# Attention a on one Trainium2 core: q, k and V in one projection by token tiles, rotation before the transpose, and the first norm shared between two steps

## The chip, the core and the metric

The kernel runs on one core of one Trainium2 chip. The metric is the device time of one execution in microseconds (us). Before the change it is 843.65 us, the median of three runs (843.44 to 843.74). All differences below are against this kernel.

The engines are TensorE (PE in the profile, PEld for its weight loads), VectorE (DVE), ScalarE (ACT), GpSimd (POOL) and SyncE (SP, here only DMA issues). Each runs its own instructions in program order and waits for others by semaphores.

## What is computed

The input is x of 16 x 256 x 128 (16 batches, 256 tokens, width 128), all in f32. Four layers follow each other, each with a residual: attention a, an expert layer, attention b, and the expert layer again.

```python
x = x + attn_a(layernorm(x), wq, wk, wv)     # one head of width 128, rotated q and k
x = x + ffn(layernorm(x), ...)               # 8 experts of width 512, one per token by argmax
x = x + attn_b(layernorm(x), ...)            # 16 causal heads of width 64
x = x + ffn(layernorm(x), ...)               # the same experts
```

The change touches attention a and, in small things, where the second norm's output is put:

```python
q = x @ wq.T; k = x @ wk.T; v = x @ wv.T
te, to = t[..., 0::2], t[..., 1::2]          # t is q or k
re = te * cos + to * sin
ro = -te * sin + to * cos                    # interleaved again
scores = qr @ kr.T / sqrt(128)
attn = softmax(scores); return attn @ v
```

## The kernel before, in words

A batch is two token tiles of 128 tokens (TPB = 2). Attention a (`attn_a` on each engine: POOL L344, ACT L419, DVE L639, PE L1050) is a software pipeline, written out as 21 steps s = 0 to 20. In step s each engine does its part for several batches at once, always in the same written order, so the order on an engine is fixed by the source:

- batch s: first norm. VectorE takes the statistics (L605, L612, L617, tile `varA`), GpSimd makes `rstdA` from them (L317, a power of -0.5), and VectorE applies the norm to two tiles (L628, tile `lnA`) near the step's end.
- batch s - 1: TensorE transposes `lnA` (L1057), ScalarE copies it (L425, `xnT`), and TensorE projects it with `WQK`, which holds wq, wq with neighbouring columns swapped, wk, and wk swapped (L1083, four products of 256 columns; the profile counts each f32 product as two). So q and k come transposed, width on the partitions, and their swapped copies beside them. VectorE multiplies q and k with the cosines out of PSUM (L695, in the program's names `w1b<-PS,ROPE`), ScalarE copies the swapped ones (L438) and GpSimd multiplies that copy with the sines (L355, `w1b<-XY,ROPE`, 512 elements in each partition). VectorE adds both (L730, `qk<-w1b`). V is a product of its own at the end of TensorE's step (L1113), which ScalarE copies (L468).
- batch s - 2: scores (L1091), row maxima (L707, `mxa`), their negative times the scale (L718, `nba`), and exp with the row sums as a by-product (L460).
- batch s - 3: transposes of the probabilities (L1071), their copy (L433), the product with V (L1106), and the reciprocal of the sums (L664, `ria`).
- batch s - 4: residual into `X` (L657), then the statistics of the second norm (`statsF`, `mvF`, `varF`), `rstdF` on GpSimd (L317, ahead of `rstdA` in the same step), VectorE's bias `nbF` (L699), ScalarE's normalised tiles `lnF` (L447).
- batch s - 5: ScalarE copies `lnF` into `TOK` (L453), from which the rows are later scattered to the experts; transposes (L1040) and the router's product (L1046), logits (L635).

VectorE's whole step from s = 4 on, in order: L657 (X), L664 (ria), L605 of batch s (statsA), L605 of s - 4 (statsF), L612 (mvF), L612 (mvA), L617 (varF), L617 (varA), L695 (cosines), L699 (nbF), L707 (mxa), L635 (logits), L718 (nba), L628 (lnA), L730 (the add). GpSimd's: rstdF, rstdA, L355. From s = 13 to 15 the 28 instructions of the first routing are woven into VectorE's steps at marked places (`part()`), and from s = 15 on GpSimd issues the scatters (L322) behind its step. TensorE gets 20 idle products at the start and some in steps 18 to 20 (`keep_clock`, L1035). The expert layer follows.

Of the kernel before, what the change touches and what calls it, by code (L numbers as in the profile page):

```python
# [34 lines left out]
SCALE_A = float(1.0 / np.sqrt(np.float32(D)))  # L35
# [55 lines left out]

def expert_steps(step, first=0, beside=None):
# [11 lines left out]
def build(nc, ids, x, wqk_a, wv_a, rope, w_q, w_k, wv_b, w_o, W1, b1t, W2, b2, Wr, br, cst, out):  # L104
    ctx = ExitStack()
    with ctx:
# [33 lines left out]
        for n in "AFB":  # L140
# [3 lines left out]
                "out": LN["A"]["out"] if n == "B" else sb(f"ln{n}", [P, 2, TPB, D]),  # L144
# [15 lines left out]
        va = sb("va", [P, 2, TPB, D])  # L160
        nbF = sb("nbF", [P, 2, TPB])
        mxa, nba, rsa, ria = (sb(n, [P, 2, TPB]) for n in ("mxa", "nba", "rsa", "ria"))
# [54 lines left out]
        (a_xT_ps, a_xT, a_qk_ps, a_qks, a_sin, a_rot, a_rope, a_v_ps, a_v, a_scores, a_max, a_nb, a_exp, a_rinv, a_pT_ps, a_pT,  # L217
         a_out_ps, a_x) = (sem("a_" + n) for n in (
             "xT_ps", "xT", "qk_ps", "qks", "sin", "rot", "rope", "v_ps", "v", "scores", "max", "nb", "exp", "rinv", "pT_ps", "pT",
             "out_ps", "x"))  # L220

        r_xT_ps, r_xT, r_tok, r_lg_ps, r_lg = (sem("r_" + n) for n in ("xT_ps", "xT", "tok", "lg_ps", "lg"))
# [27 lines left out]
        def _(sp):  # L250
# [57 lines left out]
        def _(pool):  # L308
# [17 lines left out]
            def before_scatters(k):  # L326
                pool.wait_ge(r_step, STEPS * (k + 1))
                pool.wait_ge(r_tok, GB * (k + 1))
                pool.wait_ge(s_xs0, 64)
# [14 lines left out]
            def attn_a(s, u):  # L344
                if has(s - 4):
                    rstd(LN["F"], s - 4, u)
                if has(s):
                    rstd(LN["A"], s, u)
                b = s - 1
                if has(b):  # L350
                    pool.wait_ge(a_qks, b + 1)
                    wait(pool, a_rope, b)
                    if fixed(b) and b == 0:
                        pool.wait_ge(s_wa, 48)
                    nc.gpsimd.tensor_tensor(rot[:, 1, :], qks[:, :], ROPE[:, 1, :], ALU.mult).then_inc(a_sin, 1)  # L355

            peeled(attn_a, 0, ROUTE0_AT - 1)
# [13 lines left out]
            def attn_b(s, u, more=None):  # L371
                hb, fb, gb, v = s - 1, s - 2, s - 3, (u + 1) % 2
                for q in range(QUADS):
# [39 lines left out]
        def _(act):  # L413
# [5 lines left out]
            def attn_a(s, u, beside=None):  # L419
                v = (u + 1) % 2  # L420
                b = s - 1
                if has(b):
                    act.wait_ge(a_xT_ps, b + 1)
                    wait(act, a_v_ps, b - 1)
# [17 lines left out]
                if has(b):  # L442

                    act.wait_ge(s_nbF, b + 1)
                    wait(act, r_xT_ps, b - 1)
                    for i in range(TPB):
                        last = nc.scalar.activation(LN["F"]["out"][:, u, i, :], X[:, ds(TPB * b + i), :], ACT.Identity,  # L447
                                                    bias=nbF[:, u, i:i + 1], scale=LN["F"]["rstd"][:, u, i:i + 1])
                    last.then_inc(LN["F"]["s_out"], 1)
                b = s - 5  # L450
                if has(b):
                    act.wait_ge(LN["F"]["s_out"], b + 1)
                    nc.scalar.copy(TOK[:, ds(TPB * b, TPB), 0:D], LN["F"]["out"][:, v, :, :]).then_inc(r_tok, 1)  # L453
                b = s - 2
                if has(b):
                    act.wait_ge(a_nb, b + 1)
                    wait(act, a_pT_ps, b - 1)
                    wait(act, a_rinv, b - 1)
                    for i in range(TPB):
                        last = nc.scalar.activation(pa[:, u, i, :], PS[:, 2, i * M:(i + 1) * M], ACT.Exp,  # L460
                                                    bias=nba[:, u, i:i + 1], scale=SCALE_A,
                                                    accum_out=rsa[:, u, i:i + 1])
                    last.then_inc(a_exp, 1)
                b = s - 1
                if has(b):
                    act.wait_ge(a_v_ps, b + 1)
                    wait(act, a_out_ps, b - 1)
                    nc.scalar.copy(va[:, v, :, :], PS[:, 5, 0:TPB * D].rearrange("p (t d) -> p t d", t=TPB)).then_inc(a_v, 1)  # L468
# [128 lines left out]
        def _(dve):  # L597
            nc.vector.memset(idle[:, :], 0.0).then_inc(s_idle, 1)
# [26 lines left out]
            def norm_apply(ln, n, tile, slot):  # L625
                dve.wait_ge(ln["s_rstd"], n + 1)
                for i in range(TPB):
                    last = nc.vector.tensor_scalar(ln["out"][:, slot, i, :], X[:, ds(tile + i), :],  # L628
# [10 lines left out]
            def attn_a(s, u, parts=()):  # L639
# [6 lines left out]
                if fixed(s) and s == 0:  # L646
                    dve.wait_ge(s_x0, 16)
                if fixed(s) and s == 2:
                    dve.wait_ge(s_x1, 16)
                if fixed(s) and s == 4:  # L650
                    dve.wait_ge(s_x2, 16)
                b = s - 4
                if has(b):
                    dve.wait_ge(a_out_ps, b + 1)
                    dve.wait_ge(a_rinv, b + 1)
                    for i in range(TPB):
                        last = nc.vector.scalar_tensor_tensor(  # L657
                            out=X[:, ds(TPB * b + i), :], in0=PS[:, 6, i * D:(i + 1) * D], scalar=ria[:, u, i:i + 1],
                            in1=X[:, ds(TPB * b + i), :], op0=ALU.mult, op1=ALU.add)
                    last.then_inc(a_x, 1)  # L660
                b = s - 3
                if has(b):
# [724 lines left out]
```

## Time and profile before

| what | value |
|---|---|
| median of three runs | 843.65 us |
| the profiled execution's own time | 843.43 us |
| its span, first to last instruction | 841.6 us |
| TensorE busy, mean granted clock | 798.5 us (95%), 0.994 |
| VectorE, ScalarE, GpSimd busy | 620.1, 566.4, 436.7 us |
| 22619 instructions | 6860 products on TensorE |

Times in all views are us from the span's start. A busy TensorE is not a TensorE at its peak, since its products are pipelined and their ends are modelled. Idle time of an engine matters only where its instruction is the last that something waits for. Attention a fills about the first 115 us of the span, attention b the stretch from some 230 to 730 us, the two expert layers the rest.

### The profile page before, as it was taken

Reading aid. Unit: us, or ns where it says so; the run is one execution under the profiler, and the core shown is the slowest. Engines: PE = TensorE matmul, PEld = TensorE weight load, DVE = VectorE, ACT = ScalarE, POOL = GpSimd, SP = SyncE. Lnnn points to the kernel's source line nnn. Section 1 sums busy time; section 2 is a strip of 40 time slices with the busy share of each in tenths; the row PEclk is TensorE's granted clock in tenths of the full one; section 3 lists DMA queues with packets and bytes.
Section 4 is the critical chain, followed back from the end, with each engine's and each line's share of the span. In section 5 each row is a group of like instructions: output and inputs, shape, how many; then the busy total and the mean of one; then the engine's idle time right before and its main releaser. Section 6 shows DMA issues by size and latency. Waiting matters only on the chain.

```text
span 841.6 us, 22619 instructions
## 1 busy us (share of the span) xinstructions
PE 798.5 (95%) x6860; PEld 691.8 (82%) x6860; DVE 620.1 (74%) x2697; ACT 566.4 (67%) x2044; POOL 436.7 (52%) x771
## 2 busy tenths in 40 slices
PE   7999869999899999999999999999999999899993
PEld 5888738999788888888888888888778888589992
DVE  4889766667667777777777777887767777576665
ACT  2676635666677777777777777767767777356661
POOL 3343655677544544544544444444884444237772
PEclk9999999999999999999999999999999999999997
DMA  9930021313200000000000000000020000003135
GB/s 322 336 124 2 16 76 65 118 54 99 70 2 2 2 2 2 2 2 2 2 2 2 2 2 2 2 3 1 27 96 5 2 2 3 1 23 124 54 102 168
DMA packets 26358, 40.45 MB, mean 48 GB/s; under 512 B 4672, under 2 KB 18112, under 8 KB 25216
## 3 DMA queue, kind: packets, MB, share of 16 engines
q1 hardware_dynamic: 19136, 27.71, 10.1%
q0 software_dynamic: 4992, 10.27, 3.8%
q8 instruction: 56, 0.92, 0.5%
q10 hardware_dynamic: 2112, 1.05, 0.5%
q14 instruction: 62, 0.51, 0.2%
HBM read 20.58 MB, written 18.43 MB: 46 GB/s over the span
## 4 chain that ended last, share of the span: by engine, by line
PE 74%; DVE 9%; POOL 7%; issue 5%; DMA 2%; ACT 1%; DVEq 1%; SPq 0%; POOLq 0%
PE PS L1192 11%; PE PS L1204 10%; PE PS L1183 10%; PE PS L1156 9%; PE PS L1147 9%; PE PS L1235 6%; PE PS L1028 5%; PE PS L1030 5%; PE PS L1029 5%; POOL xs_dram L322 3%; POOL w1b L355 2%; PE PS L1139 1%; POOL rstdA L317 1%; POOL pb L381 1%; DVE qk L730 1%
## 5 line engine op out<-in xcount | busy, mean ns | idle before, releaser
L379 POOL TENSOR_SCALAR pb<-pb,rib 128x128 f32<-128x128 f32 x256 | 95.3, 372 | 247.0 <-DVE rib L907 246.4
L898 DVE CUSTOM_DVE_ANT_0 PS<-PS,CST 128x128 f32<-128x128 f32 (+1 forms) x512 | 169.0, 382 | 60.5 <-PE PS L1204 60.5
L912 DVE COPY pT<-PS 128x384 f32<-128x384 f32 x256 | 140.1, 554 | 37.8 <-PE PS L1183 37.6
L523 ACT ACTIVATE pb<-PS,nbb 128x128 f32<-128x128 f32 x256 | 94.9, 371 | 96.1 <-DVE nbb L898 92.3
L496 ACT ACTIVATE yT<-PS,w1b 128x128 f32<-128x128 f32 x368 | 104.9, 368 | 61.0 <-PE PS L1147 61.0
L381 POOL TENSOR_SCALAR pb<-pb,rib 128x256 f32<-128x256 f32 x256 | 122.3, 478 | 0.0
L1183 PE MATMUL PS<-CST,pb 128*128 128x128 f32 x768 | 117.5, 278 | 4.4 <-POOL pb L381 3.9
L525 ACT ACTIVATE pb<-PS,nbb 128x256 f32<-128x256 f32 x256 | 121.2, 473 | 0.0
L1183 PEld LDWEIGHTS PS<-CST,pb 128*128 128x128 f32 x768 | 85.9, 142 | 28.0 <-issue 23.0
L338 POOL DMA_INDIRECT yt_dram<-XY x92 | 90.7, 986 | 32.6 <-issue 24.4
L1192 PE MATMUL PS<-pT,vb 128*64 128x256 f32 (+1 forms) x1024 | 103.2, 339 | 2.1 <-DVE pT L912 1.8
L1204 PE MATMUL PS<-qk 64*128 64x128 f32 (+1 forms) x1024 | 101.3, 337 | 0.0
L1156 PE MATMUL PS<-yT 128*128 128x128 f32 x736 | 97.5, 275 | 0.5 <-ACT yT L496 0.3
L1147 PE MATMUL PS<-pb,w1b 128*128 128x128 f32 x736 | 97.4, 275 | 0.4 <-issue 0.4
L1192 PEld LDWEIGHTS PS<-pT,vb 128*64 128x64 f32 x1024 | 62.2, 136 | 39.7 <-ACT qk L532 9.1
L532 ACT COPY qk<-PS 128x512 f32<-128x512 f32 x128 | 75.6, 591 | 25.9 <-PE PS L1030 25.5
L1156 PEld LDWEIGHTS PS<-yT 128*128 128x128 f32 x736 | 89.6, 192 | 1.0 <-ACT yT L496 0.9
L322 POOL DMA_INDIRECT xs_dram<-TOK,POS x64 | 65.6, 1026 | 47.1 <-DVE xs L850 29.0
L1147 PEld LDWEIGHTS PS<-pb,w1b 128*128 128x128 f32 x736 | 89.4, 192 | 0.6 <-issue 0.6
L1204 PEld LDWEIGHTS PS<-qk 64*128 64x128 f32 x1024 | 72.5, 187 | 14.0 <-issue 10.8
L1028 PE MATMUL PS<-xh,WQKh 128*128 128x256 f32 x256 | 77.8, 304 | 0.9 <-ACT qk L532 0.9
L1030 PE MATMUL PS<-xh,WQKl 128*128 128x256 f32 x256 | 72.5, 283 | 0.0
(134 smaller groups left out, 1690.9 us busy)
## 6 DMA issues: line engine op xcount, KB each, us to landing
xs_dram<-XY SPq DMA_DIRECT2D x4, 1483.5 KB, 13.1
XY<-xs_dram SPq DMA_DIRECT2D x4, 1225.5 KB, 6.1
W1S<-in_W SPq DMA_DIRECT2D x1, 2048.0 KB, 20.3
W2S<-in_W SPq DMA_DIRECT2D x4, 512.0 KB, 8.1
out_dram<-X SPq DMA_DIRECT2D x6, 256.0 KB, 2.4
yt_dram<-XY POOLq DMA_INDIRECT x92, 2.6
XY<-xs_dram SPq DMA_DIRECT2D x4, 258.0 KB, 2.6
xs_dram<-TOK,POS POOLq DMA_INDIRECT x64, 2.3
```

What stands on the lines that cost most here:

```text
L381: nc.gpsimd.tensor_scalar(pb[:, i, P:3 * P], pb[:, i, P:3 * P], rib[:, i, 1:2], 1.0, ALU.mult, ALU.mult).then_inc(b_p, 1)
L496: last = nc.scalar.activation(hT[:, v, c, :], PS[:, v, c * P:(c + 1) * P], ACT.Gelu, bias=w1b1[:, v, F + c:F + c + 1])
L525: nc.scalar.activation(pb[:, r, P:3 * P], PS[:, bank, P:3 * P], ACT.Exp, bias=nbb[:, r, 1:2], scale=-1.0, accum_out=rsb[:, r, 1:2]).then_i ...
L898: last = nc.vector.tensor_tensor_reduce(ps, ps, CST[:, m:m + c1 - c0], -SCALE_B, HIGHEST, ALU.add, ALU.min, nbb[:, hh % 4, c0 // P:c0 // P ...
L912: nc.vector.tensor_copy(pT[:, hh % 4, :], PS[:, bank, 0:3 * P]).then_inc(b_pT, 1)
L1028: mm(ps, one_pass(lhs[0]), one_pass(rhs[0]), start=True, stop=False)
L1030: return mm(ps, one_pass(lhs[1]), one_pass(rhs[0]), start=False, stop=True)
L1147: last = mm(PS[:, v, c * P:(c + 1) * P], w1b1[:, v, c * P:(c + 1) * P], xsT[:, v, :], start=True, stop=True)
L1156: last = mm(PS[:, 6 + w, 0:D], hT[:, w, c, :], w2b2[:, r, c * D:(c + 1) * D], start=c == 0, stop=c == FC - 1)
L1183: last = tr(PS[:, bank, c * P:(c + 1) * P], pb[:, hh % 4, c * P:(c + 1) * P], ident)
L1192: last = mm(PS[i * DK:(i + 1) * DK, bank, k0:M], vb[:, v if b is hb else u, c, hh * DK:(hh + 1) * DK], pT[:, hh % 4, a0:a1], start=c == 0, ...
L1204: last = mm(PS[:, S_BANKS[2 * half + i], c0:c0 + k1], qk[r, half, 0, q0:q0 + P], qk[r, half, 1, 0:k1], start=True, stop=True)
```

## The change

Projection: for each token tile one product of 384 columns with `WQKV` (wq, wk, wv side by side, the even columns of q and k ahead of the odd ones) gives q, k and V with the tokens on the partitions. The swapped copies of the weights are gone; the two halves of a row take their part. ScalarE copies q and k of both tiles (512 elements) out of PSUM; VectorE multiplies this copy in SBUF with the cosines, GpSimd makes the sine part from it in two instructions of 256 elements, VectorE adds. The sum is then transposed on TensorE (four transposes, at the beginning of the next step), copied by ScalarE, and only then come the scores. The scale is in the tables, so the maxima are negated at once and `nba` as an own instruction goes. V has a column of ones, so that the product with V gives the row sums in its last column (129 columns); their reciprocal moves to the beginning of the next step.

Norm: the statistics of batch s + 1 are taken in step s, and the norm of batch s is applied at the beginning of step s. A step s = -1 is put in front. The second norm's output goes straight into `TOK` in both attentions; the copies L453 and L387 go.

VectorE's step after, in order: reciprocal, lnA of batch s (two), statsA of s + 1 (two), X (two), statsF (two), mvF, mvA, varF, varA, nbF, negated maxima, cosines, logits, add. GpSimd's: rstdF, rstdA of s + 1, sines (two). TensorE's: transposes of lnA (s - 1), of TOK (s - 5), of the probabilities (s - 3), of q and k (s - 2), projection (s - 1), scores (s - 2), router (s - 5), product with V (s - 3).

```diff
-            sp.dma_start(WQK[:, :, :], wqk_a).then_inc(s_wa, 16)
-            sp.dma_start(ROPE[:, :, :], rope).then_inc(s_wa, 16)
+            sp.dma_start(WQKV[:, :], wqkv_a).then_inc(s_wa, 16)
+            sp.dma_start(ROPE[:, :, :, :], rope).then_inc(s_wa, 16)
             sp.dma_start(X[:, 4:8, :], xv[:, 4:8, :]).then_inc(s_x1, 16)
-            sp.dma_start(WVA[:, :], wv_a).then_inc(s_wa, 16)
...
# GpSimd, attn_a
-                if has(s):
-                    rstd(LN["A"], s, u)
+                if has(s + 1):
+                    rstd(LN["A"], s + 1, (s + 1) % 2)
                 b = s - 1
                 if has(b):
                     pool.wait_ge(a_qks, b + 1)
                     wait(pool, a_rope, b)
...
-                    nc.gpsimd.tensor_tensor(rot[:, 1, :], qks[:, :], ROPE[:, 1, :], ALU.mult).then_inc(a_sin, 1)
+                    for h in range(2):
+                        last = nc.gpsimd.tensor_tensor(by_halves(rot[:, 1, :])[:, :, :, h, :],
+                                                       by_halves(qks)[:, :, :, 1 - h, :],
+                                                       ROPE[:, 1 + h, :, None, :].to_broadcast([P, TPB, 2, D // 2]), ALU.mult)
+                    last.then_inc(a_sin, 1)
...
# ScalarE, attn_a, behind the copy of the transposed probabilities
+                b = s - 2
+                if has(b):
+                    act.wait_ge(a_qkT_ps, b + 1)
+                    wait(act, a_scores, b)
+                    nc.scalar.copy(qkT.rearrange("p w m -> p (w m)"), PS[:, 5, :]).then_inc(a_qkT, 1)
                 b = s - 1
                 if has(b):
-                    act.wait_ge(a_qk_ps, b + 1)
+                    act.wait_ge(a_qkv_ps, b + 1)
                     wait(act, a_sin, b)
-                    nc.scalar.copy(qks[:, :], PS[:, 1, :]).then_inc(a_qks, 1)
+                    wait(act, a_rot, b)
+                    nc.scalar.copy(qks.rearrange("p (t c) -> p t c", t=TPB), PS[:, 0:TPB, 0:2 * D]).then_inc(a_qks, 1)
...
-                    nc.scalar.copy(TOK[:, ds(TPB * b, TPB), 0:D], LN["F"]["out"][:, v, :, :]).then_inc(r_tok, 1)
...
                         last = nc.scalar.activation(pa[:, u, i, :], PS[:, 2, i * M:(i + 1) * M], ACT.Exp,
-                                                    bias=nba[:, u, i:i + 1], scale=SCALE_A,
-                                                    accum_out=rsa[:, u, i:i + 1])
+                                                    bias=nba[:, u, i:i + 1])
...
# VectorE, attn_a (a = s + 1, f = s - 4)
+                if has(f):
+                    dve.wait_ge(a_out_ps, f + 1)
+                    out_ps = PS[:, 6, 0:TPB * DI].rearrange("p (t d) -> p t d", t=TPB)
+                    nc.vector.reciprocal(ria[:, u, :], out_ps[:, :, D]).then_inc(a_rinv, 1)
+                if has(s):
+                    if s >= 2:
+                        dve.wait_ge(a_xT_ps, s - 1)
+                    norm_apply(LN["A"], s, TPB * s, u)
+                if has(a):
+                    bn_stats(LN["A"], a, TPB * a, a % 2)
+                if has(f):
+                    dve.wait_ge(a_rinv, f + 1)
                     for i in range(TPB):
                         last = nc.vector.scalar_tensor_tensor(
-                            out=X[:, ds(TPB * b + i), :], in0=PS[:, 6, i * D:(i + 1) * D], scalar=ria[:, u, i:i + 1],
+                            out=X[:, ds(TPB * f + i), :], in0=out_ps[:, i, 0:D], scalar=ria[:, u, i:i + 1],
...
                     dve.wait_ge(a_x, f + 1)
                     bn_stats(LN["F"], f, TPB * f, u)
...
-                    dve.wait_ge(a_qk_ps, b + 1)
-                    nc.vector.tensor_tensor(rot[:, 0, :], PS[:, 0, :], ROPE[:, 0, :], ALU.mult).then_inc(a_rot, 1)
                 part()
                 if has(f):
                     dve.wait_ge(LN["F"]["s_rstd"], f + 1)
...
-                    nc.vector.reduce_max(mxa[:, u, :], PS[:, 2, :].rearrange("p (t m) -> p t m", t=TPB),
-                                         AX.X).then_inc(a_max, 1)
+                    nc.vector.reduce_max(nba[:, u, :], PS[:, 2, :].rearrange("p (t m) -> p t m", t=TPB),
+                                         AX.X, negate=True).then_inc(a_nb, 1)
                 part()
+                b = s - 1
+                if has(b):
+                    dve.wait_ge(a_qks, b + 1)
...
+                    nc.vector.tensor_tensor(rot[:, 0, :].rearrange("p (t g c) -> p t g c", t=TPB, g=4),
+                                            qks.rearrange("p (t g c) -> p t g c", t=TPB, g=4),
+                                            ROPE[:, 0, :, None, :].to_broadcast([P, TPB, 4, D // 2]),
+                                            ALU.mult).then_inc(a_rot, 1)
...
-                    nc.vector.tensor_scalar(nba[:, u, :], mxa[:, u, :], -SCALE_A, None, ALU.mult).then_inc(a_nb, 1)
                 part()
-                if has(s) and not (fixed(s) and s == 1):
...
-                    norm_apply(LN["A"], s, TPB * s, u)
...
# TensorE, attn_a, behind the transposes of the probabilities
+                b = s - 2
+                if has(b):
+                    pe.wait_ge(a_rope, b + 1)
+                    wait(pe, a_qkT, b)
+                    for i in range(TPB):
+                        for w in range(2):
+                            last = tr(PS[:, 5, w * M + i * P:w * M + (i + 1) * P], qkn[:, (2 * i + w) * D:(2 * i + w + 1) * D],
+                                      ident)
+                    last.then_inc(a_qkT_ps, 1)
...
-                    for i in range(2):
-                        for w in range(2):
-                            last = mm(PS[:, i, w * M:(w + 1) * M], WQK[:, 2 * w + i, :], xnT[:, v, :],
-                                      start=True, stop=True)
-                    last.then_inc(a_qk_ps, 1)
+                    wait(pe, a_v, b)
+                    for i in range(TPB):
+                        last = mm(PS[:, i, 0:3 * D], xnT[:, v, i * P:(i + 1) * P], WQKV[:, :], start=True, stop=True)
+                    last.then_inc(a_qkv_ps, 1)
...
```

## Rows read from the trace of the kernel before

**Rows 1.** The stages in windows: us and count by engine, clock, DMA share, GB/s.

```profile
40.00:60.00 20.00, 19.92 (x126) 17.39 (x125) 17.44 (x78) 13.98 (x43) 7.69 (x10) 1.00 0.53 161
...
100.00:120.00 20.00, 13.46 (x79) 8.21 (x78) 10.69 (x41) 11.56 (x28) 14.12 (x16) 1.00 0.13 40
```

**Rows 2.** Chain of waits and VectorE timeline: the add that ends steps 3, 12, 16.

```profile
22.89 0.60 DVE qk L730
...
74.01 0.60 DVE qk L730
...
98.51 0.69 DVE L730 TENSOR_TENSOR qk<-w1b 128x512 f32<-128x512 f32 x1
```

**Rows 3.** VectorE in order of time through step 7: start us, us, line, operands.

```profile
39.61 0.68 DVE L730 TENSOR_TENSOR qk<-w1b 128x512 f32<-128x512 f32 x1
...
40.22 0.60 DVE L657 SCALAR_TENSOR_TENSOR X<-PS,ria,X 128x128 f32<-128x128 f32 x2
...
40.81 0.46 DVE L605 BATCH_NORM_STATS2 statsA<-X 128x6 f32<-128x128 f32 x2
...
41.19 0.46 DVE L605 BATCH_NORM_STATS2 statsF<-X 128x6 f32<-128x128 f32 x2
...
41.80 0.25 DVE L612 BATCH_NORM_AGGREGATE mvF<-statsF 128x2 f32<-128x6 f32 x2
...
42.16 0.17 DVE L617 TENSOR_SCALAR varF<-mvF 128x2 f32<-128x2 f32 x1
...
43.47 0.15 DVE L699 SCALAR_TENSOR_TENSOR nbF<-mvF,rstdF 128x2 f32<-128x2 f32 x1
...
43.72 0.69 DVE L707 TENSOR_REDUCE mxa<-PS 128x2 f32<-128x512 f32 x1
...
44.45 0.38 DVE L718 TENSOR_SCALAR nba<-mxa 128x2 f32<-128x2 f32 x1
...
44.74 0.59 DVE L628 TENSOR_SCALAR lnA<-X,mvA,rstdA 128x128 f32<-128x128 f32 x2
...
45.25 0.68 DVE L730 TENSOR_TENSOR qk<-w1b 128x512 f32<-128x512 f32 x1
```

**Rows 4.** GpSimd in order of time through the same step.

```profile
42.41 0.69 POOL L317 TENSOR_TENSOR rstdF<-varF,half 128x2 f32<-128x2 f32 x1 [3.25 <-DVE varF L617]
...
43.06 0.69 POOL L317 TENSOR_TENSOR rstdA<-varA,half 128x2 f32<-128x2 f32 x1
...
43.71 1.09 POOL L355 TENSOR_TENSOR w1b<-XY,ROPE 128x512 f32<-128x512 f32 x1
```

**Rows 5.** TensorE and ScalarE in order of time in the same step.

```profile
40.83 1.99 PE L1083 MATMUL PS<-xnT,WQK 128*128 128x256 f32 x8
...
42.66 1.03 PE L1091 MATMUL PS<-qk 128*128 128x256 f32 x4
...
44.86 0.61 PE L1113 MATMUL PS<-WVA,xnT 128*128 128x128 f32 x4
...
42.86 0.59 ACT L438 COPY XY<-PS 128x512 f32<-128x512 f32 x1 [1.29 <-PE PS L1083]
```

**Rows 6.** VectorE and GpSimd side by side in step 14.

```profile
85.16 0.29 DVE L784 TENSOR_TENSOR r_exc<-r_ps,r_exc 128x128 f32<-128x128 f32 x1
...
85.38 1.09 POOL L355 TENSOR_TENSOR w1b<-XY,ROPE 128x512 f32<-128x512 f32 x1
...
85.97 0.64 DVE L785 TENSOR_TENSOR r_exc<-r_exc,r_hot 128x128 f32<-128x128 f32 x1
```

**Rows 7.** Costliest groups: GpSimd on 128 and on 256 elements.

```profile
L379 POOL TENSOR_SCALAR pb<-pb,rib 128x128 f32<-128x128 f32 x256 | 95.3, 372 | 247.0 <-DVE rib L907 246.4
...
L381 POOL TENSOR_SCALAR pb<-pb,rib 128x256 f32<-128x256 f32 x256 | 122.3, 478 | 0.0
```

**Rows 8.** The start in order of time.

```profile
8.24 0.37 ACT L425 COPY xnT<-PS 128x256 f32<-128x256 f32 x1 [6.23 <-PE PS L1057]
...
9.52 1.99 PE L1083 MATMUL PS<-xnT,WQK 128*128 128x256 f32 x8 [1.31 <-DMA WVA<-in_wv_a]
```

More of the change, by code:

```diff
@@ L159, in build @@
         qk = sb("qk", [P, 2, 2, M])
-        va = sb("va", [P, 2, TPB, D])
+        qkn, qkT = qk[:, 0].rearrange("p a m -> p (a m)"), qk[:, 1]
+        va = sb("va", [P, 2, TPB, D + 1])
         nbF = sb("nbF", [P, 2, TPB])
-        mxa, nba, rsa, ria = (sb(n, [P, 2, TPB]) for n in ("mxa", "nba", "rsa", "ria"))
+        nba, ria = (sb(n, [P, 2, TPB]) for n in ("nba", "ria"))
         pa = lent[:, 0:2 * TPB * M].rearrange("p (a b m) -> p a b m", a=2, b=TPB)
@@ L423, in attn_a @@
                     act.wait_ge(a_xT_ps, b + 1)
-                    wait(act, a_v_ps, b - 1)
+                    wait(act, a_qkv_ps, b - 1)
                     nc.scalar.copy(xnT[:, v, :], PS[:, 4, 0:M]).then_inc(a_xT, 1)
@@ L444, in attn_a @@
                     act.wait_ge(s_nbF, b + 1)
[L445 removed]
                     for i in range(TPB):
[L447 removed]
+                        last = nc.scalar.activation(TOK[:, TPB * b + i, 0:D], X[:, ds(TPB * b + i), :], ACT.Identity,
                                                     bias=nbF[:, u, i:i + 1], scale=LN["F"]["rstd"][:, u, i:i + 1])
                     last.then_inc(LN["F"]["s_out"], 1)
[L450 to L453 removed]
                 b = s - 2
@@ L627, in norm_apply @@
                 for i in range(TPB):
-                    last = nc.vector.tensor_scalar(ln["out"][:, slot, i, :], X[:, ds(tile + i), :],
+                    to = TOK[:, tile + i, 0:D] if ln is LN["F"] else ln["out"][:, slot, i, :]
+                    last = nc.vector.tensor_scalar(to, X[:, ds(tile + i), :],
                                                    ln["mv"][:, slot, i, 0:1], ln["rstd"][:, slot, i:i + 1],
@@ L675, in attn_a @@
                 part()
-                if has(s):
-                    bn_aggr(LN["A"], s, u)
+                if has(a):
+                    bn_aggr(LN["A"], a, a % 2)
                 part()
@@ L682, in attn_a @@
                 part()
-                if has(s):
-                    norm_var(LN["A"], s, u)
+                if has(a):
+                    norm_var(LN["A"], a, a % 2)
                 part()
-                if fixed(s) and s == 1:
-                    norm_apply(LN["A"], s, TPB * s, u)
-                b = s - 1
-                if has(b):
-                    dve.wait_ge(a_qk_ps, b + 1)
-                    if fixed(b) and b == 0:
-                        dve.wait_ge(s_wa, 48)
-                    wait(dve, a_rope, b)
-                    nc.vector.tensor_tensor(rot[:, 0, :], PS[:, 0, :], ROPE[:, 0, :], ALU.mult).then_inc(a_rot, 1)
                 part()
@@ L728, in attn_a @@
                     dve.wait_ge(a_sin, b + 1)
-                    wait(dve, a_scores, b - 1)
-                    nc.vector.tensor_tensor(qk[:, v, :, :].rearrange("p a m -> p (a m)"), rot[:, 0, :], rot[:, 1, :],
-                                            ALU.add).then_inc(a_rope, 1)
+                    wait(dve, a_qkT_ps, b)
+                    nc.vector.tensor_tensor(qkn, rot[:, 0, :], rot[:, 1, :], ALU.add).then_inc(a_rope, 1)
                 part()
@@ L1105, in attn_a @@
                         for kc in range(TPB):
-                            last = mm(PS[:, 6, i * D:(i + 1) * D], pTa[:, v, kc, i * P:(i + 1) * P],
+                            last = mm(PS[:, 6, i * DI:(i + 1) * DI], pTa[:, v, kc, i * P:(i + 1) * P],
                                       va[:, v, kc, :], start=kc == 0, stop=kc == TPB - 1)
                     last.then_inc(a_out_ps, 1)
-                b = s - 1
-                if has(b):
-                    wait(pe, a_v, b)
-                    for i in range(TPB):
-                        last = mm(PS[:, 5, i * D:(i + 1) * D], xnT[:, v, i * P:(i + 1) * P], WVA[:, :],
-                                  start=True, stop=True)
-                    last.then_inc(a_v_ps, 1)
             def route(k):
@@ L1355 @@
     a = {n.replace("L0_", ""): np.asarray(v) for n, v in inputs.items()}
-    swap = np.arange(D) ^ 1
-    wq, wk = a["attn_a_wq"].T, a["attn_a_wk"].T
+    halves = np.concatenate([np.arange(0, D, 2), np.arange(1, D, 2)])
     rope, cst = tables()
```

97 lines of the change are left out of this document (39 added, 58 removed).

## The prediction, made before the changed kernel was seen

> **What bounds the kernel now.** The windows come first: through attention a TensorE is busy 19.92 of 20 us, later in the stage, where it is busy 13.46 of 20 us, its granted clock is still 1.00 [rows 1]. That looks like a stage bound by TensorE, but the chain of waits does not run over TensorE there. It goes from VectorE's add L730 through VectorE's own step to GpSimd (rstdF, rstdA, L355) and back to L730, once for each step. The adds that close steps 3 and 12 stand at 22.89 and 74.01, the one of step 16 at 98.51 [rows 2]: 5.68 us a step up to step 12.
>
> The timelines of step 7 show the loop. From the add's issue at 39.61 to varF at 42.16 VectorE takes 2.55 us without a hole; GpSimd starts rstdF 0.25 later, then come 0.65, 0.65 and 1.09 us, to 44.80; the add follows 0.45 later, at 45.25 [rows 3, 4]. The sum is 5.64, the whole step. One row says why GpSimd's end matters before the add: L718, a tiny VectorE instruction, lasts 0.38 us and ends at 44.83, just behind L355 at 44.80 [rows 3, 4]. Behind it stand only lnA (0.51) and the add. TensorE's step is as long because two loops are nearly equal: its own instructions fill 5.5 to 5.6 us.
>
> Attention b and the experts hardly touch what is changed: a copy on GpSimd and a wait there go, on engines that are not their limit. I count them at nothing, with 0.5 us either way as my bound.
>
> **TensorE, part by part.** The projection goes from 2048 to 1536 moving columns in all. Eight products took 1.83 us (40.83 to 42.66), so I take 1.83 x 0.75 = 1.37 us. V's four (up to 0.61) go, and four new transposes of 128 columns come, for which the same row stands as a bound [rows 5]; I take 0.55 for each. Net: 0.46 us less in each step, some 5.2 in place of 5.6. This is off the path unless the other loop shrinks as well.
>
> **VectorE and GpSimd, where the step is decided.** Let the add be issued at 0. All durations are those of step 7 [rows 3, 4] unless said.
>
> - To the next instruction 0.61. The reciprocal 0.07 (it stood between X and statsA and only moves). lnA, now here, 0.51. statsA 0.38.
> - X is 0.60 long, and statsF now stands directly behind it and needs its result. Such a wait on its own result costs 0.15 more: statsF ends at 41.65, and mvF is issued at 41.80. Before, ria and statsA stood in between. So 0.75, of which 0.23 is new.
> - statsF to mvF 0.61, mvF to varF 0.36. varF is issued at 3.29.
> - GpSimd: rstdF at 3.54, rstdA at 4.19, the sines at 4.84.
> - VectorE meanwhile has nothing between varA and nbF, for the cosines no longer stand there. rstdF ends at 4.23, nbF comes 0.2 later at 4.43, the maxima at 4.53, the cosines can be issued at 5.14.
> - The sines are two instructions of 256 elements. If they only share the old work they take 1.09 together. On GpSimd going from 128 to 256 elements adds 0.106 to 0.372 us [rows 7], so a second start can cost up to 0.27: 1.36. I take 1.25, nearer to the upper end because the halves are also taken in runs of 64 elements.
>
> Do sines and cosines run side by side? The cosines read q and k from SBUF now, not PSUM, so both factors lie in SBUF. Step 14 has such a pair: L785, two SBUF inputs, is issued during L355, lasts 0.64 us in place of the 0.29 of its like L784, and ends at 86.61, 0.14 behind L355's end at 86.47 [rows 6]. L718 shows the same hold [rows 3]. So I take them one behind the other: 4.84 + 1.25 + 0.55 for the cosines' elements, and 0.2 until the add is issued. That gives 6.84, rounded 6.8 us a step, whichever of the three instructions goes first.
>
> The Trainium skill (SBUF — State Buffer, "Who interferes with whom") states this as a rule: a VectorE instruction with two SBUF inputs contends with a GpSimd instruction that reads SBUF, and whoever comes second is blocked to the other's end. The trace agrees with L355 and not with rstdA: nbF, with two SBUF inputs, ran at 43.47 inside rstdA's 43.06 to 43.75. By the rule the step is 6.8, without it 6.3.
>
> Could anything else be later than this? After the add (0.68 busy and 0.06) TensorE transposes q and k (0.55), projects (1.37, end 0.16 later), ScalarE copies q and k (0.05 and 0.59): the copy is ready at 3.5, the scores at 3.7 [rows 5]. Both are earlier than the sines at 4.84 and the maxima at 4.53. The new copies on ScalarE (0.59 for the transposed q and k) stand beside a removed one and two removed reads of the sums; ScalarE stays below 4.5 us of work. So a step with the second norm lasts 6.8, a step without it is set by this path: 3.5 + 1.25 + 0.55 + 0.2 = 5.5.
>
> **The start.** The first projection waited for V's weights until 9.52 although its operand was copied at 8.61 [rows 8]. Those bytes go, and I expect it at 8.7: a gain of 0.85. It ends 1.53 later, at 10.2, the copy at 10.85, sines and cosines 2.0 later: first add at 12.85. Steps 2 and 3 at 5.5 bring it to 23.85, against 22.89: the gain is lost again, 1.0 late, because the transposes stand in front of the projection now and wait for the add.
>
> **The sum.** Steps 4 to 12: 9 x 6.8 = 61.2, so the add of step 12 stands at 85.05, 11.0 later than 74.01. In steps 13 to 15 routing instructions stand in front of nbF and fill its wait; what is left is statsF's wait and the shared reads. I take 0.5 for each of the steps 13 to 16, bounded by 0.1 and 1.1 (the whole difference of the steps before). That is 2.0. In the last four steps the reciprocal has no cover any more (about 0.25 each), and a copy of about as much goes from ScalarE: nothing, with 1 us either way. Together 13.0 us. The profiled execution took 843.43, its span 841.6; 843.4 + 13.0 = 856.4. The median of the runs is 0.2 above that execution, which I neglect.
>
> **Rivals.**
>
> 1. *Sines and cosines do not hold each other up.* For it: nbF inside rstdA. Against it: L785 and L718. Then the step is the later of 4.84 + 1.25 + 0.2 = 6.3 and 5.14 + 0.69 + 0.15 = 5.98. First add 12.3, steps 2 and 3 at 4.95, step 12's add at 22.2 + 56.7 = 78.9, 4.9 late; with 1.0 for steps 13 to 16 this gives 849.3. With sines at 1.09 it is 6.13 a step, and 847.8.
> 2. *The other side: TensorE set the step, and gets shorter.* For it: busy 19.92 of 20 us [rows 1]. Saved would be 0.46 in each of 15 steps, 6.9, and 0.85 at the start: 835.6. It decides only if the loop over VectorE and GpSimd closes in less than 5.2 us, and for no loss at all it must close within the present 5.64. My sum has 6.13 as its lowest, and the same sum gave the old step to the hundredth. I would have to be wrong about lnA or nbF.
> 3. *A half costs GpSimd as much as the whole*, because of the exchanged halves and the broadcast table. Then the sines take 2.18, the step 7.7, and with the steps around it the time is about 867. No row speaks for it, only the lack of such a pattern in the trace.
>
> **How the numbers follow.** The main case gets 0.62; its own range is 854 to 859 (6.65 to 7.0 a step, and 1 us for the end). Rival 1 gets 0.22, rival 2 0.08, rival 3 0.05. The last 0.03 is for gains at the ends that cancel the loss. The range 848 to 860 holds the main case and nearly all of rival 1. A change under 0.2%, 1.7 us, is not told from none here: faster 0.09, same 0.03, slower 0.88.
>
> **What would show it.** Right: adds of VectorE 6.8 apart in steps 5 to 12; a hole of about 0.9 on VectorE before nbF, ended by rstdF; cosines longer than their 0.69, ending behind a GpSimd instruction; TensorE idle before the transposes of q and k, waiting for the add; busy for some 5.2 us in each step, with the clock at 1.00; first projection at 8.7. Wrong: adds less than 6.1 apart, cosines of 0.69 beside the sines (rival 1), or no idle time on TensorE (rival 2).

## The result, and the profile after

The changed kernel takes 856.37 us, the median of four runs (855.73 to 857.73); the kernel before took 843.69 us beside it (843.44 to 844.88). The ratio is 1.0148, with a 95% interval from 1.0135 to 1.0160: slower by 12.7 us. The prediction was 856.4 us. The experiments were run in three batches. In the second one the kernel before took 889.37 us, with a lower granted clock in the expert layers (0.93 in 120 to 240 us in all_split, 1.00 in all_split_again, the same kernel in the third batch). Both batches ran on chip 8, and what lowered the clock is open. Each experiment is therefore read by its ratio to the kernel before in its own batch, and by the steps of attention a, which agree between the batches (5.69 and 5.68 us for cos_hole, 5.43 twice for all_split). The ratios are estimated over all runs and can differ from the quotient of two medians by up to 0.001.

The page of the kernel after, its span and the busy time of each engine:

```profile
span 854.0 us, 22411 instructions
...
PE 794.6 (93%) x6793; PEld 679.0 (80%) x6796; DVE 622.4 (73%) x2682; ACT 567.9 (66%) x2012; POOL 438.3 (51%) x771
```

The span grew by 12.4 us while TensorE's work shrank by 3.9 us and no other engine's grew by more than 2.3. The page alone does not show the loss: it lies in waits.

The kernel after in windows, with the columns of [rows 1]:

```profile
10.00:15.00 5.00, 1.29 (x8) 1.02 (x8) 2.88 (x12) 1.42 (x4) 2.27 (x3) 0.98 1.07 380
15.00:20.00 5.00, 3.73 (x12) 2.28 (x11) 2.04 (x4) 1.77 (x5) 1.92 (x3) 0.67 1.01 425
...
40.00:60.00 20.00, 15.44 (x95) 12.28 (x94) 15.15 (x60) 12.54 (x30) 8.97 (x12) 0.98 0.43 137
...
100.00:105.00 5.00, 4.87 (x20) 3.38 (x18) 3.88 (x20) 2.48 (x6) 1.04 (x2) 0.66 0.01 3
```

In 40 to 60 us TensorE is busy 15.44 us where it was 19.92 [rows 1]. With a step of 6.64 us that is 5.13 us a step. The granted clock, which was 1.00 in this stage before, falls in three short stretches, to means of 0.67, 0.74 (60 to 65 us) and 0.66 over 5 us. Such a mean mixes the two levels, 2.4 GHz at 1.00 and 1.2 GHz at 0.50.

The timeline of the kernel after, all engines: the start, then steps 6 and 7, then the add of step 12, two rows of step 15, and the add of step 16. Columns are start, length, engine, line, operands.

```profile
8.13 1.53 PE L1095 MATMUL PS<-WQKV,xnT 128*128 128x384 f32 x4 [0.55 <-ACT xnT L432]
...
10.58 1.08 POOL L322 TENSOR_TENSOR rstdA<-varA,half 128x2 f32<-128x2 f32 x1 [1.79 <-DVE varA L623]
...
12.97 0.69 DVE L733 TENSOR_TENSOR qk<-w1b 128x512 f32<-128x512 f32 x1 [1.85 <-POOL w1b L362]
...
18.70 0.68 DVE L717 TENSOR_TENSOR w1b<-XY,ROPE 128x512 f32<-128x512 f32 x1
...
24.63 0.69 DVE L733 TENSOR_TENSOR qk<-w1b 128x512 f32<-128x512 f32 x1
...
42.77 1.07 DVE L717 TENSOR_TENSOR w1b<-XY,ROPE 128x512 f32<-128x512 f32 x1
...
43.25 1.09 POOL L362 TENSOR_TENSOR w1b<-XY,ROPE 128x256 f32<-128x256 f32 x1
...
44.43 0.69 DVE L733 TENSOR_TENSOR qk<-w1b 128x512 f32<-128x512 f32 x1 [0.51 <-issue]
...
45.18 0.66 PE L1085 MATMUL PS<-CST,qk 128*128 128x128 f32 x4 [0.32 <-DVE qk L733]
...
47.74 0.17 DVE L623 TENSOR_SCALAR varF<-mvF 128x2 f32<-128x2 f32 x1
...
47.99 0.69 POOL L322 TENSOR_TENSOR rstdF<-varF,half 128x2 f32<-128x2 f32 x1 [3.65 <-DVE varF L623]
48.65 0.69 POOL L322 TENSOR_TENSOR rstdA<-varA,half 128x2 f32<-128x2 f32 x1
48.72 0.16 DVE L700 SCALAR_TENSOR_TENSOR nbF<-mvF,rstdF 128x2 f32<-128x2 f32 x1 [0.71 <-POOL rstdF L322]
...
49.30 1.69 POOL L362 TENSOR_TENSOR w1b<-XY,ROPE 128x256 f32<-128x256 f32 x2
49.41 1.07 DVE L717 TENSOR_TENSOR w1b<-XY,ROPE 128x512 f32<-128x512 f32 x1
...
50.62 0.44 PE L1042 MATMUL PS<-CST,TOK 128*128 128x128 f32 x2 [1.07 <-DVE LG L643]
51.07 0.69 DVE L733 TENSOR_TENSOR qk<-w1b 128x512 f32<-128x512 f32 x1 [0.51 <-issue]
...
84.69 0.69 DVE L733 TENSOR_TENSOR qk<-w1b 128x512 f32<-128x512 f32 x1 [0.51 <-issue]
...
101.57 2.46 PE L1095 MATMUL PS<-WQKV,xnT 128*128 128x384 f32 x4
...
104.06 0.59 ACT L451 COPY XY<-PS 128x512 f32<-128x512 f32 x1 [1.67 <-PE PS L1095]
...
111.94 0.69 DVE L733 TENSOR_TENSOR qk<-w1b 128x512 f32<-128x512 f32 x1
```

How to read it. The adds L733 stand 6.64 us apart (44.43 to 51.07), where L730 stood 5.64 apart [rows 3]. Counted from the add, varF comes at 3.31, rstdF at 3.56, rstdA at 4.22 and the sines at 4.87. The two sines fill 1.69 us, to 50.99, and the add follows 0.08 later. The cosines last 1.07 in place of the 0.68 that they took at 18.70, where no GpSimd instruction stood beside them (the sines of that step ended at 18.27). The step before shows the order inside. The cosines (42.77 to 43.84) end behind the first sine, and the second sine, issued at 43.25, lasts 1.09 us and ends at 44.34, 0.50 behind the cosines. So the three run one at a time: sine, cosines, sine. The chain of waits of the same step, kernel after, says it in its own way:

```profile
49.34 1.15 POOL w1b L362 x2
...
50.56 0.51 issue
```

### The profile page after: what moved, and what is told of

Its sections match the earlier page's. It is cut to its first block, busy times and chain, and to the rows that moved or that the text cites. A ratio compares the mean times of both kernels' runs of the same rounds, so it can differ in the third digit from the quotient of the medians.

```text
span 854.0 us, 22411 instructions
## 1 busy us (share of the span) xinstructions
PE 794.6 (93%) x6793; PEld 679.0 (80%) x6796; DVE 622.4 (73%) x2682; ACT 567.9 (66%) x2012; POOL 438.3 (51%) x771
## 3 DMA queue, kind: packets, MB, share of 16 engines
q1 hardware_dynamic: 18992, 27.25, 9.9%
## 4 chain that ended last, share of the span: by engine, by line
PE 72%; DVE 9%; POOL 8%; issue 7%; DMA 1%; ACT 1%; DVEq 1%; POOLq 0%; SPq 0%
PE PS L1196 10%; PE PS L1208 10%; PE PS L1187 10%; PE PS L1151 9%; PE PS L1160 9%; PE PS L1239 6%; PE PS L1030 5%; PE PS L1032 5%; PE PS L1031 5%; POOL xs_dram L327 3%; POOL w1b L362 2%; PE PS L1143 1%; POOL rstdA L322 1%; POOL pb L391 1%; DVE X L677 1%
## 5 line engine op out<-in xcount | busy, mean ns | idle before, releaser
L900 DVE DVE_READ_ACCUMULATOR2_ANT nbb<- 128x1 f32 x512 | 72.5, 142 | 0.0
```

The source lines that it names most:

```text
L900: last = nc.vector.tensor_tensor_reduce(ps, ps, CST[:, m:m + c1 - c0], -SCALE_B, HIGHEST, ALU.add, ALU.min, nbb[:, hh % 4, c0 // P:c0 // P ...
```

## The experiments

All edits are against the kernel after, but for the first, which is against the kernel before.

**norm_only**: the norm part alone, put into the kernel before.

```diff
-  (VectorE, at the step's end)   norm_apply(LN["A"], s, ...)
+  (VectorE, first in the step)   norm_apply(LN["A"], s, ...); bn_stats(LN["A"], s + 1, ...)
-  (GpSimd)                       rstd(LN["A"], s, u)
+  (GpSimd)                       rstd(LN["A"], s + 1, (s + 1) % 2)
```

> The kernel before with only the norm's part of the change: statistics of batch s + 1 in step s, the norm applied at the beginning of step s. Theory (the loop over VectorE and GpSimd sets the step): from the add 0.61, lnA 0.51, statsA 0.38, X and the wait of statsF for it 0.75, 0.61, 0.36, so varF at 3.22; GpSimd 0.25, 0.65, 0.65, 1.09, and 0.2 to the add: 6.0 a step in place of 5.64. Nine full steps and a little in steps 13 to 16: 847.5 us (846 to 849). Rival (lnA behind the sines was the cost, its move is a gain, and the loss of the change comes from the projection alone): 5.2 to 5.6 a step, 839 to 844 us.

Measured: 849.76 us (847.78 to 851.49) beside 843.53, ratio 1.0074 (1.0054 to 1.0094). VectorE and GpSimd in time through step 7:

```profile
41.80 0.69 DVE L728 TENSOR_TENSOR qk<-w1b 128x512 f32<-128x512 f32 x1
...
46.59 1.09 POOL L355 TENSOR_TENSOR w1b<-XY,ROPE 128x512 f32<-128x512 f32 x1
...
46.99 0.72 DVE L720 TENSOR_SCALAR nba<-mxa 128x2 f32<-128x2 f32 x1
...
47.78 0.69 DVE L728 TENSOR_TENSOR qk<-w1b 128x512 f32<-128x512 f32 x1
```

The step is 5.98, as expected. lnA stood behind GpSimd before, and it stands ahead of varF now. With it and with statsF's wait for X, varF is issued 3.24 behind the add, where it was 2.55; at the other end the add follows L355's end by 0.10 and no longer by 0.45. L720, which has two elements in a partition, lasts 0.72 us and ends with L355. The time is above what the step alone makes: steps 4 to 12 give 2.6 us, the rest comes at the start (1.2) and in steps 13 to 16 (1.6); the add of step 16 stands at 103.80, 5.3 late.

**proj_only**: the projection part alone, the norm where it was.

```diff
-                if has(s + 1):
-                    rstd(LN["A"], s + 1, (s + 1) % 2)
+                if has(s):
+                    rstd(LN["A"], s, u)
...
+                if has(s) and s != 1:          # VectorE, behind the logits, ahead of the add
+                    norm_apply(LN["A"], s, TPB * s, u)
```

> The changed kernel with the norm as it was before (statistics of batch s in step s, lnA behind the logits); the projection, the rotation and the row sums as changed. Theory: lnA goes from the beginning of the step, where it costs 0.5, to behind the sines, where it costs the same, since its VectorE instruction does not start before GpSimd is through; the step stays 6.5 to 6.7, the time 854 to 858 us. Rival (the moved norm is what costs): 845 to 850 us.

Measured: 857.37 us (853.5 to 858.89) beside 843.53, ratio 1.0161 (1.0128 to 1.0193). VectorE through step 7:

```profile
44.07 0.68 DVE L735 TENSOR_TENSOR qk<-w1b 128x512 f32<-128x512 f32 x1
...
49.60 0.83 DVE L636 TENSOR_SCALAR lnA<-X,mvA,rstdA 128x128 f32<-128x128 f32 x2
50.35 0.68 DVE L735 TENSOR_TENSOR qk<-w1b 128x512 f32<-128x512 f32 x1
```

A step of 6.28, less than I expected: lnA lies in the time in which the add waits for the held sine anyway, so it costs little there. The nine steps are 3.6 us shorter than in the kernel after. The time is not, because steps 13 to 15 take 22.5 us (81.78 to 104.26) where the kernel after takes 21.9, its add of step 3 is 0.7 later, and the 2.2 us that its add of step 16 (109.74) is ahead are lost behind it. In the step the two parts add up: 0.34 for the norm and 0.64 for the projection, of 1.00 for both. In the time they do not. The step to the third add takes 7.33 us here, with a clock of 0.86 and 0.79 in 15 to 25 us, and step 15 takes 7.56, with 0.71 in 95 to 100 us; idle2 below shows what such falls cost. So moving the norm back alone is no cure.

**cos_psum**: the cosines read q and k from PSUM again, beside ScalarE's copy.

```diff
-                                            qks.rearrange("p (t g c) -> p t g c", t=TPB, g=4),
+                                            PS[:, 0:TPB, 0:2 * D].rearrange("p t (g c) -> p t g c", g=4),
...
+                    act.wait_ge(a_rot, b + 1)     # the copy of V and the next projection wait for the cosines
+                    wait(pe, a_rot, b)
```

> The changed kernel, only that VectorE multiplies q and k with the cosines out of PSUM, behind ScalarE's copy of them, so that one of its two factors is not in SBUF; ScalarE's copy of V waits for it. Theory (cosines and sines hold each other up, about 0.5 us in each step): cosines 0.69 long, the two sines without a hole between them, step 6.1; 0.53 in each of 16 steps less at most, 848 to 851 us. Rival (no hold, the cosines only come late): step 6.6, 856 us as changed.

Measured: 850.04 us (847.76 to 851.19) beside 843.53, ratio 1.0070 (1.0051 to 1.0088). VectorE and GpSimd through step 7:

```profile
43.98 0.69 DVE L734 TENSOR_TENSOR qk<-w1b 128x512 f32<-128x512 f32 x1 [0.45 <-issue]
...
48.84 1.24 POOL L362 TENSOR_TENSOR w1b<-XY,ROPE 128x256 f32<-128x256 f32 x2
48.96 0.68 DVE L718 TENSOR_TENSOR w1b<-PS,ROPE 128x512 f32<-128x512 f32 x1
...
50.17 0.69 DVE L734 TENSOR_TENSOR qk<-w1b 128x512 f32<-128x512 f32 x1 [0.46 <-issue]
```

With one input in PSUM, cosines and sines run side by side: 0.68 and 1.24 us, nothing held, a step of 6.19. The hold is worth 0.45 us a step. By the medians of the two batches this one operand is worth half of the whole loss (6.3 of 12.7 us); the nine steps 4 to 12 give 4.0 of it, steps 13 to 16 another 1.4, and the start gives nothing (the add of step 3 stands at 25.52, again with a fall of the clock, 0.66 in 15 to 20 us).

**idle2**: two idle products of 512 columns behind TensorE's work in steps 1 to 12.

```diff
+                if 1 <= s < ROUTE0_AT:
+                    keep_clock(2, 4)
```

> The changed kernel with two idle products of 512 columns at the end of TensorE's step, in steps 1 to 12: 0.43 us more work for TensorE in each. Theory (TensorE has over 1 us free in a step of 6.64): the step stays 6.64, and the three falls of the granted clock (stretches at 0.67, 0.74 and 0.66) become fewer; 854 to 856.5 us. Rival (TensorE sets the step): 0.43 more in 12 steps, 861 us.

Measured: 855.03 us (854.75 to 856.6) beside 843.53, ratio 1.0141 (1.0124 to 1.0158). VectorE's adds, at the start and in step 7:

```profile
13.82 0.69 DVE L733 TENSOR_TENSOR qk<-w1b 128x512 f32<-128x512 f32 x1 [1.85 <-POOL w1b L362]
...
19.03 0.69 DVE L733 TENSOR_TENSOR qk<-w1b 128x512 f32<-128x512 f32 x1
...
44.05 0.69 DVE L733 TENSOR_TENSOR qk<-w1b 128x512 f32<-128x512 f32 x1 [0.50 <-issue]
...
50.70 0.69 DVE L733 TENSOR_TENSOR qk<-w1b 128x512 f32<-128x512 f32 x1 [0.51 <-issue]
```

More work on TensorE, and the same step of 6.65: TensorE does not set it. The clock's falls moved and did not go: the three of the kernel after are not there, others stand at 90 to 95 us (0.66) and 115 to 125 us (0.88, 0.78). That gives their price, since the same steps are now seen at 1.00. The step to the second add takes 5.21 us where it took 6.44 with the clock at 0.67, the step to the third is the same in both (5.21 and 5.22), and step 15 takes 5.94 (in cos_psum too) where it took 6.64 with 0.66. So the falls cost 1.23 and 0.70 us there. Not every fall costs time: step 14, in which idle2 has its fall, takes 7.45 us, and 7.44 without one, and the step of the kernel after that holds the fall at 60 to 65 us takes 6.69, against 6.64 in idle2.

**hole**: lnA put into VectorE's wait for rstdF, behind varA.

```diff
-                if has(s):                        # first in VectorE's step
-                    norm_apply(LN["A"], s, TPB * s, u)
...
                     norm_var(LN["A"], a, a % 2)
+                if has(s):
+                    norm_apply(LN["A"], s, TPB * s, u)
```

> The changed kernel, only that lnA of batch s stands behind varA, in VectorE's wait for rstdF, not at the beginning of the step. Theory: the 0.50 of lnA leaves the way from the add to varF (3.31 to 2.81) and is hidden in the wait of 0.71 before nbF; the step goes from 6.64 to 6.14, the time to 850 us (848.5 to 852). Rival (lnA is held up by GpSimd's rstdF, as L718 was by L355, or the wait does not hide it): the step stays above 6.4, 853 us or more.

Measured: 895.99 us (895.06 to 897.45) beside 889.37, ratio 1.0081 (1.0057 to 1.0105). VectorE and GpSimd through step 7:

```profile
43.89 0.69 DVE L733 TENSOR_TENSOR qk<-w1b 128x512 f32<-128x512 f32 x1 [0.51 <-issue]
...
46.88 0.60 DVE L636 TENSOR_SCALAR lnA<-X,mvA,rstdA 128x128 f32<-128x128 f32 x2
46.94 0.69 POOL L322 TENSOR_TENSOR rstdF<-varF,half 128x2 f32<-128x2 f32 x1 [3.14 <-DVE varF L623]
...
47.66 0.16 DVE L700 SCALAR_TENSOR_TENSOR nbF<-mvF,rstdF 128x2 f32<-128x2 f32 x1 [0.18 <-POOL rstdF L322]
...
50.02 0.69 DVE L733 TENSOR_TENSOR qk<-w1b 128x512 f32<-128x512 f32 x1 [0.51 <-issue]
```

A step of 6.13. The hole of 0.71 before nbF becomes 0.18; lnA at the head of the step costs its whole 0.51.

**cos_hole** and **cos_hole_again**: both edits together, in the second batch and once more in the third.

> Both edits on the changed kernel: the cosines out of PSUM, and lnA in the wait before nbF. Theory (both costs lie in one loop and add): 2.81 + 0.25 + 0.65 + 0.65 + 1.24 + 0.09 = 5.69 a step, 844.5 us (843 to 846), as the kernel before. Rival (TensorE's order becomes the bound once the loop is shorter): 5.9 or more a step, 846 to 849 us.

> Both edits (cosines out of PSUM, lnA in the wait before nbF) beside the changed kernel on one chip. Theory: 5.69 a step, so the loss of 1.5% is gone but for 0.2%; the two edits together are worth 1.3 to 1.5%. Rival (half of the loss lies elsewhere): 0.5% or more over the kernel before.

Measured: 890.03 us beside 889.37, ratio 1.0000 (0.9985 to 1.0014), and 843.86 (843.11 to 845.97) beside 844.02, ratio 0.9995 (0.9981 to 1.0010). VectorE's adds in the repeat:

```profile
38.72 0.69 DVE L734 TENSOR_TENSOR qk<-w1b 128x512 f32<-128x512 f32 x1 [0.46 <-issue]
...
44.40 0.69 DVE L734 TENSOR_TENSOR qk<-w1b 128x512 f32<-128x512 f32 x1 [0.45 <-issue]
```

5.68 us a step, the step of the kernel before. The savings in the step add up (0.45 and 0.51, together 0.96 of 6.64), and the whole loss of 1.5% is gone. The nine steps give 8.7 us of it. 2.8 come at the start, where the clock does not fall here and the add of step 3 stands at 21.80 and not 24.63, and 1.5 in steps 13 to 16. The clock is 1.00 in 15 to 20 us in both runs, while hole alone has 0.53 and cos_psum alone 0.66; why is open.

**cos_hole_sin**: in addition rstdA behind the sines on GpSimd, since its reader lnA now comes a step later.

```diff
-                if has(s + 1):
-                    rstd(LN["A"], s + 1, (s + 1) % 2)     # ahead of the sines
...
+                if has(s + 1):
+                    rstd(LN["A"], s + 1, (s + 1) % 2)     # behind them
```

> As cos_hole, and GpSimd makes rstdA of batch s + 1 behind the sines, since lnA needs it only in the next step. Theory: rstdA's 0.65 leaves GpSimd's part of the loop (5.04), and VectorE's own way is the longest now: varF at 2.81, then 0.98 to nbF, 0.08, 0.61, and 0.84 for the cosines and the wait for them: 5.3 a step; 840.5 us (839 to 842.5), faster than both kernels. Rival (GpSimd's place in the loop does not matter, something else holds the step at 5.65): 844 us.

Measured: 890.10 us (888.57 to 892.75) beside 889.37, ratio 1.0014 (1.0001 to 1.0027). VectorE and GpSimd in step 7:

```profile
48.02 1.23 POOL L360 TENSOR_TENSOR w1b<-XY,ROPE 128x256 f32<-128x256 f32 x2
48.09 0.58 DVE L701 SCALAR_TENSOR_TENSOR nbF<-mvF,rstdF 128x2 f32<-128x2 f32 x1
```

A miss: 5.59 a step (38.39 to 43.98), not 5.3. The sines start 0.65 earlier and hold nbF: two SBUF inputs, two elements, 0.58 us in place of 0.16, until the first sine ends. Maxima and cosines stand behind it. The time does not follow the step at all: step 12 ends 1.02 earlier than in cos_hole (72.26 against 73.28), and step 13 alone gives 0.86 back (8.23 against 7.37).

**all_split** and **all_split_again**: in addition the second half of statsA between X and statsF, where statsF waited for X.

```diff
                     last.then_inc(a_x, 1)
+                    if has(a):
+                        stats_a(1).then_inc(LN["A"]["s_stats"], 1)
                     dve.wait_ge(a_x, f + 1)
```

> As cos_hole_sin, and statsA's second half stands between X and statsF, so that statsF does not wait for a result just made. Theory: 0.2 less on the same way, 5.1 a step, where TensorE's own 5.2 takes over: 839.5 us (838 to 842). Rival (TensorE is the bound already in cos_hole_sin): no difference from it, 840.5 us.

> All four edits. Theory: adds 5.43 apart, 0.3 to 0.5% under the kernel before. Rival (the gain of before belongs to that chip, where the expert layers run otherwise): no difference from the kernel before.

Measured: 886.41 us (883.71 to 887.77) beside 889.37, ratio 0.9966 (0.9952 to 0.9979), and 839.64 (839.4 to 841.84) beside 844.02, ratio 0.9951 (0.9936 to 0.9967). VectorE and GpSimd of the repeat, in steps 6 and 7, and one row of step 13:

```profile
43.72 1.23 POOL L360 TENSOR_TENSOR w1b<-XY,ROPE 128x256 f32<-128x256 f32 x2
43.76 0.62 DVE L707 SCALAR_TENSOR_TENSOR nbF<-mvF,rstdF 128x2 f32<-128x2 f32 x1 [0.19 <-POOL rstdF L322]
...
45.61 0.69 DVE L740 TENSOR_TENSOR qk<-w1b 128x512 f32<-128x512 f32 x1
...
51.04 0.69 DVE L740 TENSOR_TENSOR qk<-w1b 128x512 f32<-128x512 f32 x1
...
77.22 1.14 DVE L767 TENSOR_TENSOR r_hot<-CST,r_best 128x128 bf16<-128x128 f32 x1
```

5.43 a step, with nbF still held (I had hoped for 5.1). This version beats the kernel before by 0.3 to 0.5%, and with that the kernel after by some 2%. Step 13 gives part back: 72.74 to 80.77, 8.03 us. lnA and r_hot now stand beside the sines (76.59 to 77.82) and last 0.99 and 1.14 us, and the clock is 0.86 and 0.79 in 75 to 85 us; the two were not told apart.

**all_nb**: in addition nbF's product on GpSimd, from means negated on VectorE in front of varF.

```diff
+                    nc.vector.tensor_scalar(nmF[:, u, :], LN["F"]["mv"][:, u, :, 0], -1.0, None, ALU.mult)
...
+                    nc.gpsimd.tensor_tensor(nbF[:, u, :], nmF[:, u, :], LN["F"]["rstd"][:, u, :],
+                                            ALU.mult).then_inc(s_nbF, 1)
```

> As all_split, and nbF is no longer a VectorE instruction with two SBUF inputs beside the sines: VectorE negates the means before varF, GpSimd multiplies them with rstdF, behind it. Theory (nbF was held by the first sine and lasted 0.62 in place of 0.16): VectorE's step loses the hold, GpSimd's gets one small instruction of about 0.2; adds 5.2 apart, where TensorE's own work ends, 2 us less than all_split. Rival (nbF was late for another reason, or GpSimd's small instruction costs as much): 5.4 apart, no difference.

Measured: 842.86 us (839.24 to 843.9) beside 844.02, ratio 0.9977 (0.9963 to 0.9991). Its VectorE timeline has the add of step 16 3.4 us earlier than all_split_again (99.19); the window at the start of the experts follows:

```profile
95.82 0.69 DVE L741 TENSOR_TENSOR qk<-w1b 128x512 f32<-128x512 f32 x1 [0.19 <-issue]
```

```profile
126.00:128.00 2.00, 2.00 (x10) 1.48 (x8) 1.48 (x5) 0.00 (x0) 1.70 (x2) 0.50 0.12 38
```

The steps are 5.27 apart, as expected, but the time is a miss: not shorter than all_split's. In this profile the granted clock is 0.50, the level of 1.2 GHz, just when the experts begin (eight products at 126.91 last 1.84 us, eight of the same at 128.99 in all_split_again 1.07). That goes with the loss. So do the ten runs: the three shortest (839.24 to 840.73) have a mean clock of 0.989 or 0.990, the other seven (842.31 to 843.90) 0.987. Whether the clock explains all of it stays open.

**after_again**: the kernel after in the third batch.

> The changed kernel as it is, on the chip of the following three, so that the steps of the ladder are compared on one chip. Theory: 1.5% over the kernel before, adds 6.64 apart. Rival (the 1.5% belongs to the first chip): another ratio.

Measured: 857.13 us (857.04 to 859.66) beside 844.02, ratio 1.0162 (1.0140 to 1.0184), adds 6.64 apart. The result stands.

## Why the prediction was right

The time and the mechanism were right. That the time is met to 0.1 us is luck, though: the terms of the sum were off by 0.7 to 1.1 us each, two of them one way and two the other. Adds are taken from the timelines, where those of steps 3 and 12 before stand at 22.81 and 73.93, 0.08 earlier than in the chain's rows [rows 2].

| term | predicted, later by | measured |
|---|---|---|
| up to the add of step 3 | 1.0 | 1.8 (24.63 against 22.81) |
| steps 4 to 12 | 10.0 (6.8 a step) | 8.9 (60.06 against 51.12; 6.67 a step) |
| steps 13 to 16 | 2.0 | 2.7 (27.25 against 24.58) |
| behind step 16 | 0 (1 either way) | -1.0 |
| span | 13.0 | 12.4 |

- *The front of the loop*: right to 0.03. varF, rstdF, rstdA and the sines were put at 3.29, 3.54, 4.19 and 4.84 and came at 3.31, 3.56, 4.22 and 4.87. lnA ahead of varF and the wait of statsF for X cost what they were put at; the hole on VectorE before nbF was 0.71 and not about 0.9. What the order costs is shown by hole: with lnA in that hole the step is 0.51 shorter.
- *The hold*: right, and shown by cos_psum. The Trainium skill (SBUF — State Buffer, "Who interferes with whom") says that a VectorE instruction with two SBUF inputs and a reading GpSimd instruction exclude each other, the later one being blocked. The rows agree for sines and cosines, and for nbF beside a sine (0.58 and 0.62 us). For rstdA they agree in one order only. nbF took 0.16 inside it (48.65 to 49.34). But rstdA is itself blocked when the cosines come first: it lasts 1.08 us at 10.58, issued 0.16 behind them, and 0.69 in cos_psum, where they read PSUM.
- *Its size* was put 0.1 too high: 0.55 expected, 0.45 by cos_psum. The order I left open is sine, cosines, sine. The sines themselves were put at 1.25 and take 1.24 wide. And the add is issued 0.08 behind GpSimd's end, not 0.2. These, less the 0.03 of the front, make 6.64 out of 6.84.
- *Rival 1* (no hold, 6.3 or 6.13 a step) is the kernel cos_psum, and there the step is 6.19. So its sum was right too, for a kernel that is not this one.
- *Rival 2* (TensorE set the step) falls: TensorE is busy 5.13 a step where 5.2 was predicted, and it idles 1.07 and 0.32 us in each, the 0.32 waiting for the add. With two more products a step (idle2) the step is the same.
- *Rival 3* falls: the sines take 1.24 and not 2.18.
- *The clock at 1.00* was wrong. That is the one step of the prediction that failed in kind and not in size. The first projection came earlier than said (8.13, not 8.7), the first add at 12.97 about as said (12.85). But TensorE was then busy 1.29 of 5 us, and the next window has a clock of 0.67. The step to the second add took 6.44 us where I had put 5.5; at the full clock it is 5.21 (idle2), and so is the step after it, so 5.5 was itself too much. In step 15 a projection at the lower level lasts 2.46 us (in 100 to 105 us, clock 0.66) and ScalarE's copy waits 1.67 for it. By idle2 the two falls cost 1.23 and 0.70 us. The second is what steps 13 to 16 cost above their term; the first, less the 0.6 by which the two steps of the start were put too high and with 0.1 for the first add, is the 0.8 of the start. idle2 was not made for this: it has two more products in steps 1 to 12, and the price is read from steps that are otherwise the same.
- *Attention b and the experts*: nothing, as said. The loss stands already in attention a, and the last 1.0 is won back behind step 16. Half of it is back when the first expert product starts (141.67 against 128.74, 12.9 late). By which instructions was not followed up.

## What to carry to other kernels

Work out the loop through the engines from issue to issue, and put each moved instruction on it by its place, not by its length: the same 0.5 us of lnA cost 0.51 at the head of the step and next to nothing in a wait further down, and 3.9 us less work on TensorE bought nothing. When an operand moves from PSUM to SBUF, look at which GpSimd instruction runs beside its reader; here that one operand cost 0.45 of the 1.00 us that each step lost. And when a loop is shortened, ask which tiny instruction will now stand beside a long one, and whether the granted clock will stay up: one fall at the start cost 1.23 us, more than two steps' worth of the hold.

## What the hardware showed that was not expected

- A pair of GpSimd instructions lets a waiting VectorE instruction in between its two instructions: the second sine then lasts 1.09 us for its half of the work. The hold goes both ways.
- The price of a hold is that of the other's remaining time, whatever the size of the held one: two elements took 0.58 us (cos_hole_sin), 0.62 (all_split) and, with one SBUF input only, 0.72 (norm_only).
- rstdF and rstdA, 0.69 us each on two elements, were not seen to hold a VectorE instruction: nbF took 0.16 inside rstdA, lnA's pair 0.60 beside rstdF in hole, and the first cosines of after_again 0.69 inside rstdA. The other way round it does not hold: behind cosines with two SBUF inputs rstdA lasts 1.08 us (after and idle2).
- TensorE's clock fell in a stage where TensorE was busy 15.44 of 20 us, and stayed at 1.00 in the kernel before where it was busy 13.46 of 20 [rows 1]. Nor does the gap just before tell: TensorE was idle for 3.71, 3.08 and 3.07 us ahead of the first transposes of q and k in after, after_again and hole, where the clock fell, and for 3.44 us in idle2, where it did not. What decides it stays open.
